# A fused Mamba-style block and gated feed-forward on one core: float32 decay matrices and values turned into float16 halves, with four engine orders rewritten

## What is computed

```python
xn  = layernorm(x)                                   # x: (2, 2048, 512), float32
z, xs, B, C, dt = split(xn @ in_proj_w)              # 1024, 1024, 64, 64, 16 columns
v   = silu(causal_conv1d(xs, taps=4))                # 16 heads of 64
k, q = elu(B) + 1, elu(C) + 1
a   = exp(-softplus(dt + dt_bias) * exp(A_log))      # decay of each head and position
# state h = a*h + k v ;  y = q h      (done in chunks)
y   = (ssd(q, k, v, a) + D*v); y = rmsnorm(y)*norm_scale*silu(z)
ffn = hadamard(silu(gate(xn)) * up(xn)) @ W_down.T   # 512 -> 2048 -> 512, with sign/scale vectors
out = x + y @ out_proj_w + ffn
```

## Time and profile before

| | |
|---|---|
| median of 3 runs | 2012.38 us (2010.58 to 2012.64) |
| profiled execution, its own time | 2010.72 us |
| its span, first to last instruction | 2009.0 us |
| mean granted clock | 0.969 |
| PE, DVE, ACT, POOL busy | 94%, 73%, 50%, 7% of the span |
| one block of the loop | 110.77 us |

### The profile page before, as it was taken

One profiled execution on the slowest core, in us unless ns is written; L12 is line 12 of the kernel. 1 busy time (PEld: TensorE's weight loads), 2 busy tenths in 40 slices (PEclk: granted clock), 3 DMA queues, 4 the chain that ended last, 5 costly groups with the idle time before them and its releaser, 6 DMA issues.

```text
span 2009.0 us, 39344 instructions
## 1 busy us (share of the span) xinstructions
PE 1881.8 (94%) x13425; PEld 1340.0 (67%) x13426; DVE 1465.2 (73%) x3291; ACT 1013.3 (50%) x2243; POOL 140.7 (7%) x142
## 2 busy tenths in 40 slices
...
DMA packets 147828, 107.13 MB, mean 53 GB/s; under 512 B 110031, under 2 KB 111159, under 8 KB 147255
## 3 DMA queue, kind: packets, MB, share of 16 engines
...
## 4 chain that ended last, share of the span: by engine, by line
PE 89%; DVE 2%; DVEq 1%; ACT 1%; issue 0%; SPq 0%; DMA 0%; ACTq 0%
PE bank L804 87%; PE bank L871 1%; DVEq L512 1%; PE bank L625 0%; DVE wd L414 0%; DVE wug L525 0%; DVE big L414 0%; ACT wd L359 0%; ACT wo L377 0%; DVEq L485 0%; DVEq L422 0%; PE bank L848 0%; PE bank L849 0%; DVE wo L415 0%; PE bank L616 0%
## 5 line engine op out<-in xcount | busy, mean ns | idle before, releaser
L804 PE MATMUL bank<-xnT,wug 128*128 128x256 f16 x6144 | 705.4, 273 | 0.0
L804 PEld LDWEIGHTS bank<-xnT,wug 128*128 128x128 f16 x6144 | 601.1, 98 | 99.8
L804 PE MATMUL bank<-wd,h 128*128 128x512 f16 x1536 | 371.0, 379 | 0.0
L804 PEld LDWEIGHTS bank<-wd,h 128*128 128x128 f16 x1536 | 148.3, 100 | 157.2 <-issue 3.4
L804 PE MATMUL bank<-wi,xnT 128*128 128x512 f16 (+1 forms) x1152 | 204.2, 330 | 16.4 <-DMA xnT<-cvx 16.4
L963 ACT ACTIVATE tg<-bank,gate_scale 128x256 f32<-128x256 f32 x256 | 119.7, 467 | 175.1 <-PE bank L804 139.6
L1056 POOL TENSOR_TENSOR vw<-v,dec 128x512 f32<-128x512 f32 x64 | 73.9, 1154 | 1829.2 <-ACT v L1006 1374.6
L1012 ACT ACTIVATE Mx<-Mx,cs_own 128x128 f32<-128x128 f32 x512 | 162.1, 389 | 49.0 <-DMA Mx<-cs_rows 49.0
L1140 DVE SCALAR_TENSOR_TENSOR cvx<-xc,conv,cvx 128x256 f32<-128x256 f32 x384 | 169.1, 481 | 14.9 <-issue 0.4
L804 PE MATMUL bank<-xnT,wi 128*128 128x256 f16 x1536 | 172.9, 273 | 0.0
L804 PEld LDWEIGHTS bank<-wi,xnT 128*128 128x128 f16 x1152 | 101.5, 99 | 104.6 <-issue 17.2
...
## 6 DMA issues: line engine op xcount, KB each, us to landing
Mx<-cs_rows SPq DMA_DIRECT2D x128, 256.0 KB, 3.5
...
```

Of the source, the lines that this page charges most:

```text
L804: ins = nc.tensor.matmul(out, lhsT, rhs, start=first and n == 0, stop=last and n == len(pairs) - 1)
```

## The change

- **Decay matrices in halves.** After `dec`, ACT makes `M_hi` (step `mh`) and DVE `M_lo` (step `ml`), 8 each a block. `M_hi[0]` lies in `kq`, and `M_hi[q]` in the upper half of `M[q-1]`, so that `mh(q)` waits for `ml(q-1)`; `M_lo[q]` lies in the lower half of `M[q]`.
- **`itr` in float16.** For each head three matmuls in place of the float32 one.
- **v split first, then turned.** ACT `th` and DVE `tl` (4 each) make halves of the convolution's result; SP's `td` turns each with a DMA transpose (8 a block) into `v16`. `vt` is gone, on PE and ACT. Conv tile n+2 (`xb`) now waits for `v_turned[n]`, since its buffer holds the low half.
- **POOL.** `vw` first adds the two halves of v (one more operation), and `sd` takes over the decay of the state that `st` had done on DVE.
- **Small things.** The `halo` copies go from DVE's `cv` to ACT's `xp` and `xb`; ACT's scaling by `S_V` in `cs` and DVE's by `S_Y` in `ssq` are folded into constants; the halves of y lie in other buffers, and the last of them wait until chunk 0 has been turned.
- **All five lists are new.**

```diff
-bc F0 xp0 xp1 xp2 F1 qk F2 cs D0 vt0 xp3 vt1 F3 F4 vt2 G D1 D2 F5 F6 int00 vt3 int01 D3 F7 D4 itr00 D5 F8 st00
+bc xp0 xp1 F0 qk F1 cs F2 xp2 xp3 D0 G D1 F3 int00 F4 D2 F5 F6 D3 F7 F8 D4 int01 itr00 D5 st00 itr01 F9 D6
...
-vw00 vw01 vw10 vw11
+sd00 vw00 vw01 vw10 sd01 sd10 sd11 vw11
...
-store bw bd00 bd01 bd02 xin bd03 bd10 bd11 bd12 bd13 yd00 res yd01 yd10 yd11 xd
+store bw td0 bd00 bd01 bd02 td1 bd03 td2 td3 bd10 bd11 xin bd12 bd13 yd00 yd01 yd10 yd11 res xd
...
+                        for u, src in enumerate((v_hi[n % 2], v_lo[n % 2])):
+                            sp.dma_start(v16[:, 2 * n:2 * n + 2, :, u, :].rearrange("p c t d -> p (c t) d"), src, transpose=True).then_inc(v_turned[n], 16)
...
-                            hd = 8 * hf + n
-                            ins = products(o[:, n * HD:(n + 1) * HD],
-                                           [(M[2 * hf + n // 4][:, n % 4, :], v[:, c, hd * HD:(hd + 1) * HD])])
+                            hd, q = 8 * hf + n, 2 * hf + n // 4
+                            ins = products(o[:, n * HD:(n + 1) * HD], three(lambda u: (M_hi, M_lo)[u][q][:, n % 4, :],
+                                                                           lambda u: v16[:, hd // 2, c, u, hd % 2 * HD:(hd % 2 + 1) * HD]))
...
-                            act.wait_ge(ring_filled, (i + 1) * NR + filled(f"vt{n - 2}"))
+                            act.wait_ge(v_turned[n - 2], (i + 1) * 2 * 16)
+                        nc.scalar.activation(halo[:, 2 * n:2 * n + 2, :], xc[n % 2][:, :, TB:TB + TAPS - 1], ACT.Copy)
...
+                    elif k == "mh":
...
+                            act.wait_ge(M_ready, (i + 1) * 8 + 4 * c + q)
+                        act.wait_ge(M_whole, (i + 1) * 8 + 4 * c + q + 1)
+                        nc.scalar.activation(M_hi[q], M[q][:, :, :], ACT.Copy).then_inc(M_high, 1)
...
+                        pool.tensor_tensor(by_tile(vd[:, :]), v16[:, 4 * hf:4 * hf + 4, c, 0, :], v16[:, 4 * hf:4 * hf + 4, c, 1, :], ALU.add)
...
+                    elif k == "ml":
+                        c, q = at
+                        dve.wait_ge(M_high, (i + 1) * 8 + 4 * c + q + 1)
+                        nc.vector.tensor_tensor(M_lo[q], M[q][:, :, :], M_hi[q], ALU.subtract).then_inc(M_ready, 1)
+                    elif k == "tl":
+                        n = at[0]
+                        dve.wait_ge(v_high, (i + 1) * 4 + n + 1)
+                        nc.vector.scalar_tensor_tensor(v_lo[n % 2], cv[n % 2].rearrange("p c t -> p (c t)"), S_V, v_hi[n % 2], ALU.mult, ALU.subtract).then_inc(v_split, 1)
...
-                        nc.vector.tensor_tensor(half.rearrange("p (h d) -> p h d", d=HD), half.rearrange("p (h d) -> p h d", d=HD),
-                                                bcast(dec3[:, 2, c, 8 * hf:8 * hf + 8], HD), ALU.mult)
-                        dve.drain()
+                        dve.wait_ge(state_faded, i * 4 + 2 * c + hf + 1)
                         nc.vector.scalar_tensor_tensor(half, o[:, :], 1.0 / PEAK, half, ALU.mult, ALU.add).then_inc(dve_emptied, 1)
```

More of the change, by code:

```diff
@@ L44 @@
 Y_SCALE = PEAK / 1024
+Y_FOLD = 0.5 * Y_SCALE / (PEAK * XN_SCALE)
 LOW = 2.0 ** 11
 GROUP_PEAK = PEAK / 32
+C_M = 1.0 / (NS * PEAK)
 WI_GROUPS = [((0, DI), 0), ((DI, DI), 2), ((BC0, 2 * NS), 4), ((BC0 + 2 * NS, NH), 5)]
 PE_STEPS = """
-bc F0 xp0 xp1 xp2 F1 qk F2 cs D0 vt0 xp3 vt1 F3 F4 vt2 G D1 D2 F5 F6 int00 vt3 int01 D3 F7 D4 itr00 D5 F8 st00
-D6 F9 itr01 D7 F10 F11 z00 st01 int10 D8 itr10 D9 F12 z01 F13 int11 D10 itr11 st10 z10 F14 D11 z11 D12 F15 D13
-O0 D14 st11 D15 O1
+bc xp0 xp1 F0 qk F1 cs F2 xp2 xp3 D0 G D1 F3 int00 F4 D2 F5 F6 D3 F7 F8 D4 int01 itr00 D5 st00 itr01 F9 D6
@@ L58 @@
+st01 F10 z00 D7 F11 int10 D8 F12 z01 itr10 D9 F13 int11 D10 z10 st10 itr11 F14 z11 D11 D12 F15 O0 D13 D14 st11
+D15 O1
 """.split()
 ACT_STEPS = """
-elu F0 xp0 xb0 xp1 xb1 xp2 sv0 qk F1 H0 F2 sv1 cs xb2 kh vt0 H1 H2 xp3 sv2 F3 vt1 xb3 H3 F4 vt2 dec00 dec01
-sv3 F5 H4 dec02 H5 F6 vt3 F7 dec03 vh00 H6 dec10 H7 F8 dec11 H8 F9 vh01 H9 sh00 ssq0 F10 dec12 z00 dec13 H10
-vh10 F11 sh01 z01 F12 H11 F13 yh00 ssq1 H12 xh0 yh01 H13 F14 sh10 vh11 xh1 z10 yh10 z11 H14 yh11 F15 H15 sh11
+elu xp0 xb0 xp1 xb1 F0 sv0 kh qk th0 H0 cs F1 sv1 F2 H1 H2 xp2 th1 xb2 xp3 dec00 sv2 F3 th2 xb3 H3 F4 dec01
@@ L63 @@
+sv3 H4 th3 F5 mh00 dec02 mh01 H5 F6 mh02 dec03 H6 vh00 F7 F8 mh03 H7 sh00 H8 vh01 dec10 F9 ssq0 F10 dec11 H9
+z00 dec12 H10 F11 mh10 sh01 vh10 mh11 F12 dec13 mh12 mh13 z01 H11 yh00 H12 vh11 yh01 F13 ssq1 z10 xh0 xh1 H13
+F14 yh10 z11 sh10 H14 F15 yh11 H15 sh11
 """.split()
 DVE_STEPS = """
-fin bc F0 elu cv0 cv1 sv0 L0 F1 F2 sv1 qk cv2 L1 L2 sv2 F3 L3 F4 G cv3 dec00 dec01 sv3 kl F5 L4 L5 dec02 F6
-lna int00 F7 vl00 L6 itr00 lnb dec03 F8 L7 st00 F9 L8 int01 sl00 L9 itr01 dec10 dec11 vl01 F10 ssq0 int10
@@ L67 @@
-dec12 st01 z00 L10 F11 vl10 sl01 itr10 z01 dec13 L11 int11 F12 itr11 lnc F13 yl00 L12 st10 yl01 ssq1 z10 L13
-F14 yl10 z11 xl0 yl11 L14 xl1 F15 vl11 L15 sl10 st11 sl11
+bc fin elu cv0 F0 sv0 cv1 tl0 L0 F1 F2 qk sv1 L1 L2 tl1 cv2 G dec00 sv2 F3 tl2 cv3 F4 sv3 L3 kl tl3 F5 ml00
+dec01 dec02 ml01 L4 L5 F6 int00 L6 ml02 vl00 dec03 F7 ml03 itr00 st00 F8 int01 L7 itr01 vl01 sl00 L8 dec10 F9
+lna F10 lnb ssq0 L9 st01 dec11 ml10 lnc ml11 L10 sl01 F11 int10 z00 dec12 dec13 vl10 ml12 F12 itr10 z01 ml13
+int11 L11 yl00 itr11 yl01 L12 F13 ssq1 z10 st10 F14 L13 z11 yl10 xl0 F15 yl11 L14 vl11 sl10 L15 xl1 st11 sl11
@@ L154, in program @@
         h_scale = sb("h_scale", [P, KF])
-        scal = sb("scal", [P, 10])
-        S_BC, S_DT, S_Z, S_Y, S_OUT, S_K, S_V, S_G, S_INT, S_Q = (scal[:, n:n + 1] for n in range(10))
+        scal = sb("scal", [P, 11])
+        S_BC, S_DT, S_Z, S_Y, S_OUT, S_K, S_V, S_G, S_INT, S_Q, S_ITR = (scal[:, n:n + 1] for n in range(11))
         WS_UG, WS_DP, SU_UG, SU_DP, NORM, CONVW, CONVB = 0, 32, 36, 40, 56, 64, 96
@@ L758, in body @@
                         sp.dma_start(res[:, :, :], x_v[i]).then_inc(res_loaded, 16)
+                    elif k == "td":
+                        n = at[0]
+                        if n == 0 and not first:
+                            for c in range(NT):
+                                sp.wait_ge(yT_loaded[c], i * 4 * 16)
+                                sp.sem_inc(turns, 1)
+                        sp.wait_ge(v_split, i * 4 + n + 1)
+                        sp.sem_inc(turns, 1)
+                        for u, src in enumerate((v_hi[n % 2], v_lo[n % 2])):
+                            sp.dma_start(v16[:, 2 * n:2 * n + 2, :, u, :].rearrange("p c t d -> p (c t) d"), src, transpose=True).then_inc(v_turned[n], 16)
                     elif k == "yd":
@@ L1027, in body @@
                         act.wait_ge(yg_ready, (i + 1) * 4 + 2 * c + hf + 1)
-                        nc.scalar.activation(y_hi[c][hf], v[:, c, hf * 512:(hf + 1) * 512], ACT.Copy).then_inc(y_high, 1)
+                        if c == 1 and hf == 1:
+                            act.wait_ge(yT_loaded[0], (i + 1) * 4 * 16)
+                        nc.scalar.activation(by_tile(y_hi[c][hf]), y[c][hf], ACT.Copy).then_inc(y_high, 1)
                     elif k == "xh":
```

121 lines of the change are left out of this document (76 added, 45 removed).

## The result

The changed kernel takes 2037.32 us (median of 4 runs, 2034.19 to 2039.80), the kernel before beside it 2011.48 us (4 runs, 2010.42 to 2012.64). The ratio is 1.0128, with a 95% interval of 1.0115 to 1.0140: slower by 1.3%, where 3.0% faster was forecast. Its profiled execution took 2037.41 us, its span 2035.4.

What follows compares the result with a forecast made beforehand. PE was taken to bound the kernel without waiting: 5.9 us a block saved less 2.2 us of waits is 3.7, over 16 blocks 59 us, so 2010.72 becomes 1951 us, 3.0% less. Range 1913 to 1984 us.

Steps and rivals of the forecast that it cites:

- What leaves and comes to PE: PE's itr and vt: 24 float16 matmuls at 29 ns save 1.03 us per itr; with vt gone, 5.9 us a block.
- rival of 55 ns and more: PE's narrow itr matmuls cost 55 ns or more; PE saves 3.4 us a block, waits shrink to 1.0; 1972 us; chance 0.12.
- a pace of one load in 107 ns: PE's itr weight loads take 107 ns each, 1.6 us a block slower, 2036 us; chance 0.02 of the narrow-matmul rival's 0.12.
- The turning of v: SP's DMA transposes: issue 1.20 to 1.27 us, landing after 2.6; a pair is in v16 some 3.8 us after its tl.
- rival of a late convolution: Late pairs of v start cv2, cv3 and int00 late; slower than before, 2040 us at 1.8 us a block lost; chance 0.06.
- d: Lateness of v's transposed pairs: costs about d at int00, d - 1 at xb2; 2.35 us eats the net 3.7 us.
- The first part of DVE: DVE's queue up to F6: six more splits less the copies; F6 ends at 41.1 us, so PE waits 0.3 at F8.
- What comes to DVE: Twelve splits add 7.3 us a block; state products (3.0) and small copies (1.3) leave; net +2.7 us on 81.5 busy.
- POOL's nine new microseconds: POOL gets four sums of v's halves and four state products a block: about +9 us on 8.6, with room.
- Where PE will wait: PE waits at F8 0.3, st01 0.7, st10 0.5 and itr11 0.7 us: together 2.2 us a block.
- sign of being wrong: Wrong if itr takes 1.3 us or more, PE waits over 4 us a block, or a wait comes in the tail at bc.
- the forecast case: PE stays the bound and waits 1 to 4 us a block; 1951 us; chance 0.59.

Runs made afterwards that it cites:

- late_state_product: Changed kernel with one more wait: POOL's first state product of a block waits until DVE has finished L0, off the taps of cv1; 2038.27 us, ratio to before 1.0146.
- small_pool: Changed kernel with POOL's operations cut to 32 of 512 columns, DVE adding POOL's other result in int; 1980.89 us, ratio to before 0.9842.
- no_sum: Changed kernel without POOL's sum of the halves of v, its two products reading the high half alone; 2017.29 us (one run).
- filled_wait: Changed kernel with six more matmuls of 512 columns, into a bank nobody reads, on PE just ahead of st10; 2034.81 us (one run).
- locks_avoided: Changed kernel with POOL's first state product held until DVE's L0 is done and vw10 until dec10 is done; 2033.19 us, ratio to before 1.0119.
- order c: Changed kernel's instructions with the lists in a third other order, made from step times of two reordered runs; 1959.84 us, ratio to before 0.9734.
- orders a and b: Changed kernel's same instructions with the lists in two other orders, the second with both sd00 and sd01 early on POOL; 2021.12 and 1977.23 us (one run each).

## Why the prediction was wrong

**What leaves and comes to PE: right.** `itr` costs 0.69 us (0.70 forecast), 29 ns a matmul, at the lower bound. `vt` is gone. The block without waits is 112.4 - 7.4 = 105.0 us by the sum below (104.9 forecast). The rival of 55 ns and more did not happen, nor did a pace of one load in 107 ns, the figure that the Trainium skill gives in "TensorE: Matmul & The Clock Gate", section "LDWEIGHTS (loading the stationary operand)": a load passes every 29 ns, while its own record lasts 98 ns. That rival's 2036 us is the measured time to 1 us by chance alone. The streaming time of a load, which the prediction worked out from three lengths, is not shown by this; only the pace is.

**The turning of v: about 1 us too short at its end.** A transpose lands 2.7 to 2.9 us after its issue in the median (2.6 forecast). But the second issue of the last pair takes 1.46 to 2.30 us in the 16 blocks (1.27 forecast), and POOL starts 4.4 to 5.2 us after the end of `tl3`, where 3.8 were counted: 4.9 in the block shown. The rival of a late convolution did not come in its own form: `late_state_product` shows that 0.8 us at `tl0` are worth nothing. Its other half, a late pair that holds `int00`, did come, at d near 1 us. No run shortens the landing, so its price is open.

**The first part of DVE: nearly right.** `F6` was forecast to end 41.1 us into the block and ends at 41.6; PE's start of `F8` is 0.69 us late instead of 0.3.

**What comes to DVE: the term that failed first.** "Net +2.7 us" was 5.0. Of these, 2.9 us a block are 46.8 us over the loop in which DVE stands behind POOL; the rest, 2.1, is under the forecast. The prediction gave POOL's nine new microseconds a price only through `int00`'s wait (1.3 forecast, 1.95 measured in the block shown, 1.8 in the mean of 16). POOL's three operations there are as forecast (3.3 us from 1512.77 to 1516.11, 3.4 forecast); they start 1.1 us late, with the pair of v. The trace of before held the row that should have raised the question: POOL's first product has a mean of 1154 ns and its twin on the same tile 1039. With the lists of the change, `small_pool` puts POOL's whole share at 56 us, two thirds of the 86 by which the forecast missed; `no_sum` puts the sum's part of it at 20.

**Where PE will wait: the step that failed.** "Together 2.2 us a block" was 7.4 in the block shown; the waits alone are 5.2 us a block in the mean of the loop (83 / 16). That is over the 4 us that the prediction itself named as a sign of being wrong, and its other sign, a wait of PE at `bc`, came in 12 blocks. The places were the right ones, each too small, and `bc`, the two other `itr` and the half clock were left out:

| start in PE's list | forecast | measured, start to start |
|---|---|---|
| `F8` | 0.3 | 0.69 |
| `st01` | 0.7 | 1.73 |
| `st10` | 0.5 | 1.50 |
| `itr11` | 0.7 | 1.11 |
| `bc`, `itr01`, `itr10` | 0 | 0.7 |
| `itr11` and `F14` at half clock | 0 | 1.65 |

They sum to 7.4. But they are not terms that can be taken away one by one, and treating them so was the deeper error. PE is on the chain for only 27.8 of 112.4 us; behind it follow the last pair of v, POOL, 53.3 us of DVE's queue, and SP's transposes, and PE's waits are what this round leaves over. The runs bear that out: `filled_wait` filled a wait off the chain and took away the half clock, and the time stayed; `late_state_product` gained 0.8 us in the part where PE holds the chain, and nothing came of it; `no_sum` shortened a link by 20 us in the loop and the time fell by 20; `locks_avoided` pulled DVE 1.44 us forward at one place and had most of it taken back at the next. A forecast should have added up the whole round, with DVE's drains and with POOL beside it, and compared that with PE; instead it kept PE as the bound and put small waits on top.

**The rivals.** The slower side was given 0.09, by a late convolution and slow loads. The mechanism that came was none of them: PE was no longer the bound. It was inside the forecast case, which capped it at 4 us a block without a reason.

**What the change is worth.** Less work on PE is worth what was forecast, if the order lets it through: order c is at 1959.8 us, 9 above the forecast of 1951. That does not save the forecast, which was made for the lists of the change; that c comes near it is in part luck, as its own waits are other ones. The loss against the kernel before comes from the five lists that the change brought (the title counts four), together with the work that it put on POOL beside DVE. How the 77 us of order c divide between fewer collisions and better-placed waits is not settled, but collisions alone do not decide: orders a and b, with the same 3260 instructions, keep DVE busy for 1583.9 and 1575.7 us of their runs instead of 1551.8, and are still 16 and 60 us faster. In order c DVE's operations are too long by 24 us in the loop instead of 46.8, and its `int` steps wait 10.4 us for POOL instead of 28.7; both together are 41 us of DVE's time, but the runs above show that such sums do not pass through one to one.
